# A new order for the first iterations, the routed rows in four parts, and a new order of iterations 13 and 14 in a gated-delta and expert layer

## The reference

```
mixed = silu(causal_conv(xn @ w_qkv))           # q, k: 16 heads; v: 32 heads, of 128
q, k = l2norm(q), l2norm(k); beta = sigmoid(xn @ w_b); g = -exp(A_log)*softplus(xn @ w_a + dt_bias)
step: St = St*exp(g); delta = (v - k.St)*beta; St = St + k delta; o = (q/sqrt(128)).St
attn = (rmsnorm(o)*norm_weight*silu(xn @ w_z)) @ w_out
ffn  = sum of 2 of 8 experts, weighted, + (silu(xn @ w_gate)*(xn @ w_up)) @ w_down   # shared, 1024 wide
out  = x + attn + ffn
```

## Time and profile before

| | us |
|---|---|
| three runs | 1098.22, 1091.68, 1098.17 (median 1098.17) |
| profiled execution, its own time | 1106.24 |
| its span, first to last instruction | 1104.3 |
| busy: TensorE / VectorE / ScalarE / GpSimd | 1030.0 / 800.5 / 633.9 / 519.3 |
| mean granted TensorE clock | 0.98 |

### The profile page before, as it was taken

The page is one execution under the profiler, slowest core; times in us unless marked ns, Lnnn a source line. Parts: engine busy times, 40 slices in busy tenths (PEclk is TensorE's granted clock), DMA queues, the critical chain, the costliest instruction groups (busy, mean ns, idle before and its releaser), DMA issues.

```text
span 1104.3 us, 22254 instructions
## 1 busy us (share of the span) xinstructions
PE 1030.0 (93%) x8190; PEld 789.7 (72%) x8190; DVE 800.5 (72%) x1469; ACT 633.9 (57%) x1176; POOL 519.3 (47%) x1140
## 2 busy tenths in 40 slices
PE   4889999999789999999999999999999999996897
PEld 4665666578476877777777778777777778783776
DVE  4552332275769898989889898989888988897444
ACT  4341222234557777666767576777767676774453
POOL 4500000266455557383847465564738374735610
PEclk9989999999879999999999999999999999998999
DMA  9933111151132333415152334233241514332121
GB/s 325 398 114 111 48 34 59 54 160 26 44 120 37 125 50 113 97 65 123 46 116 68 96 74 125 44 119 67 96 104 58 123 57 105 75 97 42 24 47 48
DMA packets 183513, 103.16 MB, mean 93 GB/s; under 512 B 155632, under 2 KB 169584, under 8 KB 180080
## 3 DMA queue, kind: packets, MB, share of 16 engines
q1 hardware_dynamic: 181872, 97.55, 32.1%
q0 software_dynamic: 1536, 4.20, 1.1%
HBM read 79.77 MB, written 21.95 MB: 92 GB/s over the span
## 4 chain that ended last, share of the span: by engine, by line
PE 57%; DVE 8%; ACT 7%; issue 4%; POOL 3%; DMA 1%; SPq 0%; ACTq 0%; DVEq 0%
PE rg L1585 9%; PE pj L1416 6%; PE pj L1418 5%; PE pj L1417 5%; PE rg L1568 5%; PE rg L1552 5%; PE rg L1486 4%; DVE nm L1294 3%; PE rg L1560 3%; PE rg L1569 2%; DVE shared_down_or_conv L1257 2%; ACT vn L1229 2%; ACT sqk L1183 2%; PE rg L1488 2%; PE rg L1531 2%
## 5 line engine op out<-in xcount | busy, mean ns | idle before, releaser
L1085 POOL TENSOR_TENSOR rows<-rows,shared_down_or_conv 128x126 f32<-128x126 f32 (+22 forms) x496 | 187.7, 378 | 239.1 <-DMA shared_down_or_conv<-n_scratch 201.5
L1257 DVE SCALAR_TENSOR_TENSOR shared_down_or_conv<-pj,taps,shared_down_or_conv 128x510 f32<-128x510 f32 x372 | 275.5, 744 | 27.5 <-ACT shared_down_or_conv L1135 18.8
L1088 POOL TENSOR_TENSOR rows<-rows 128x126 f32<-128x126 f32 (+22 forms) x496 | 194.8, 393 | 38.9
L1416 PE MATMUL pj<-xhi,whi 128*128 128x512 f32 x376 | 164.1, 437 | 2.4 <-POOL wlo L1065 1.4
L1294 DVE SCALAR_TENSOR_TENSOR nm<-rg,wneg,hidden_or_decays 128x512 f32<-128x512 f32 (+1 forms) x256 | 139.5, 609 | 15.9 <-PE rg L1488 14.1
L1418 PE MATMUL pj<-xhi,wlo 128*128 128x512 f32 x376 | 149.9, 399 | 0.0
L1417 PE MATMUL pj<-xlo,whi 128*128 128x512 f32 x376 | 149.8, 398 | 0.0
L1135 ACT ACTIVATE shared_down_or_conv<-pj,taps 128x512 f32<-128x512 f32 x124 | 85.0, 686 | 108.0 <-PE pj L1418 106.4
L1585 PE MATMUL rg<-wo,gated 128*128 128x256 f32 x512 | 130.6, 391 | 0.1
L1585 PEld LDWEIGHTS rg<-wo,gated 128*128 128x128 f32 x512 | 95.0, 192 | 15.1 <-issue 1.3
L1416 PEld LDWEIGHTS pj<-xhi,whi 128*128 128x128 f32 x376 | 71.5, 190 | 42.7 <-issue 24.4
(11 more groups left out here) (238 smaller groups left out, 1991.3 us busy)
## 6 DMA issues: line engine op xcount, KB each, us to landing
hidden_or_decays<-eg_scratch SPq DMA_DIRECT2D x16, 1536.0 KB, 8.0
wraw<-w_heads SPq DMA_DIRECT2D x16, 776.0 KB, 4.5
w1a<-w_up SPq DMA_DIRECT2D x9, 1024.0 KB, 7.7
shared_down_or_conv<-n_scratch SPq DMA_DIRECT2D x32, 256.0 KB, 4.0
w2a<-w_down SPq DMA_DIRECT2D x8, 512.0 KB
wo<-w_out SPq DMA_DIRECT2D x16, 256.0 KB
n_scratch<-nm SPq DMA_DIRECT2D x64, 64.0 KB
rt_scratch<-shared_down_or_conv SPq DMA_DIRECT2D x32, 128.0 KB, 2.3
```

The source lines that it names most:

```text
L1085: gp.tensor_tensor(tmp, rb[:, 0:r, t:t + 1].to_broadcast([P, r, w]), nb[:, t:t + 1, t + 1:].to_broadcast([P, r, w]), ALU.mult).then_inc(el ...
L1088: gp.tensor_tensor(rb[:, 0:r, t + 1:], rb[:, 0:r, t + 1:], tmp, ALU.add).then_inc(elim, 1)
L1257: v.scalar_tensor_tensor(out=y, in0=it.pbank[item][:, :, 0:S - s], scalar=taps[par][:, piece(j)[0], KS - 1 - s:KS - s], in1=y, op0=ALU.mul ...
L1416: te.matmul(bank, whi[par][w], xhi[:, k, cols], start=(k == 0), stop=False)
```

## The change

- Iteration -1: on TensorE, K3 moves ahead of H1 and VT0 to VT3 behind P3. D0 to D3 and E0 to E3 of group 1 are done here and not in iteration 0.
- The 16 row adds become MIX0 to MIX3 of four rows. The first three wait for 12 rows and stand in iteration -1, the last stands behind P4 of iteration 0. GpSimd fetches rows 5 to 11 in iteration -1 and rows 12 to 15 at the start of iteration 0, ahead of the weight split.
- Iteration 0 begins with SQ and K0 to K3, so K3 comes before P4; LA1 to LB2 stand between the first pieces.
- Iteration 13: K2 and K3 move ahead of LA1, and VectorE does D3 ahead of K1.
- Iteration 14: P5 to P7 stand between LA1, LA2, LB1 and LB2, and Z3 behind OUT5. P4's convolution moves behind K3 on VectorE.
- `blocks_out` of group 15 moves behind all of `blocks_back` of group 14, as in all other iterations.

```
+            FIRST_ROWS = 12
                 -1: (
-                    ("K0 G0 K1 H0 G1 K2 H1 K3 P4 G2 H2 P5 G3 H3 P6 DN0 P7 DN1 G4 H4 P0 VT0 VT1 G5 H5 P1 VT2 VT3 G6 H6 P2 "
-                     "G7 H7 P3 DN2 DN3").split(),
-                    ("G0 W G1 P4 G2 P5 S4 G3 P6 S5 SK P7 S6 G4 S7 P0 VT0 VT1 G5 P1 S0 VT2 VT3 G6 P2 S1 G7 P3 S2 S3").split(),
-                    ("K0 K1 H0 K2 H1 K3 P4 H2 P5 H3 P6 DN0 P7 DN1 H4 P0 H5 P1 H6 P2 H7 P3 DN2 DN3").split(),
+                    ("K0 K1 G0 K2 H0 K3 G1 H1 P4 G2 H2 P5 G3 H3 P6 DN0 P7 DN1 G4 H4 P0 G5 H5 P1 G6 H6 G7 H7 P2 P3 "
+                     "VT0 VT1 VT2 VT3 DN2 DN3").split(),
+                    ("G0 W G1 P4 G2 P5 S4 G3 P6 S5 SK P7 S6 G4 S7 P0 E0 G5 P1 S0 G6 S1 G7 P2 P3 E1 S2 VT0 VT1 VT2 VT3 "
+                     "S3 E2 E3").split(),
+                    ("K0 K1 K2 H0 K3 H1 P4 H2 P5 H3 P6 DN0 P7 DN1 H4 D0 P0 H5 MIX0 P1 H6 MIX1 H7 D1 P2 P3 D2 DN2 D3 MIX2 "
+                     "DN3").split(),
                 0: (
-                    ("Z0 Z1 P4 P5 SQ Z2 K0 P6 Z3 K1 K2 P7 P0 LA1 K3 LA2 LB1 P1 LB2 U1_0 U1_1 N21_0 N21_1 P2 U2_0 U2_1 "
-                     "VT0 P3 O0 VT1 O1 VT2 O2 O3 VT3").split(),
+                    ("SQ K0 Z0 K1 Z1 LA1 K2 Z2 LA2 K3 Z3 LB1 P4 LB2 P5 U1_0 U1_1 P6 N21_0 N21_1 P7 U2_0 U2_1 P0 O0 P1 O1 "
+                     "VT0 P2 VT1 P3 O2 O3 VT2 VT3").split(),
...
-                    ("D0 P4 D1 D2 P5 SQ D3 K0 P6 K1 K2 P7 K3 MIX N21_0 N21_1 P0 P1 P2 O0 P3 O1 O2 O3").split(),
+                    ("SQ K0 K1 K2 K3 P4 MIX3 P5 N21_0 N21_1 P6 P7 P0 O0 P1 O1 P2 P3 O2 O3").split(),
                 NG - 3: (
-                    ("SO Z0 P4 Z1 SQ Z2 K0 OUT0 K1 OUT1 Z3 OUT2 P5 P6 P7 LA1 K2 OUT3 LA2 K3 LB1 OUT4 OUT5 LB2 P0 OUT6 "
+                    ("SO Z0 P4 Z1 SQ Z2 K0 OUT0 K1 OUT1 Z3 K2 P5 K3 P6 OUT2 P7 LA1 OUT3 LA2 OUT4 LB1 OUT5 LB2 P0 OUT6 "
...
-                    ("D0 SO D1 SQ P4 K0 OUT0 OUT1 D2 K1 D3 OUT2 P5 K2 OUT3 K3 P6 OUT4 OUT5 P7 OUT6 N21_0 P0 N21_1 P1 P2 "
+                    ("D0 SO D1 SQ P4 K0 OUT0 OUT1 D2 D3 K1 K2 K3 OUT2 P5 OUT3 P6 OUT4 OUT5 P7 OUT6 N21_0 P0 N21_1 P1 P2 "
                      "OUT7 P3 O0 O1 O2 O3").split(),
                 NG - 2: (
-                    ("P4 Z0 SO SQ Z1 P5 K0 K1 K2 K3 LA1 Z2 OUT0 P6 OUT1 OUT2 Z3 OUT3 OUT4 LA2 P7 LB1 OUT5 OUT6 LB2 U1_0 "
-                     "U1_1 N21_0 N21_1 OUT7 U2_0 U2_1 VT0 VT1 O0 O1 O2 VT2 VT3 O3").split(),
+                    ("P4 Z0 SO SQ Z1 K0 K1 K2 K3 LA1 Z2 OUT0 LA2 P5 OUT1 LB1 P6 OUT2 LB2 P7 OUT3 U1_0 U1_1 N21_0 OUT4 "
+                     "N21_1 OUT5 Z3 U2_0 U2_1 OUT6 VT0 VT1 OUT7 O0 O1 O2 VT2 VT3 O3").split(),
...
-                    ("D0 D1 SO P4 SQ D2 D3 K0 K1 K2 K3 P5 OUT0 P6 OUT1 OUT2 OUT3 OUT4 OUT5 OUT6 N21_0 N21_1 P7 OUT7 O0 "
+                    ("D0 D1 SO D2 SQ D3 K0 K1 K2 K3 P4 OUT0 P5 OUT1 P6 OUT2 P7 OUT3 N21_0 OUT4 N21_1 OUT5 OUT6 OUT7 O0 "
                      "O1 O2 O3").split(),
@@ SyncE
                     turned_back(2, tc2, turned_in)
-                    if n == NG - 2:
-                        blocks_out(n + 1, 1 - it.odd)
                     sp.wait_ge(r_out, 32 * n + 32)
...
-                        if b != NG - 2:
-                            blocks_out(b + 1, 1 - it.odd)
+                        blocks_out(b + 1, 1 - it.odd)
@@ GpSimd
                     if it.b == -1:
                         gather(range(0, 5))
+                    elif it.b == 0:
+                        gp.wait_ge(gathered, FIRST_ROWS * 16)
+                        gather(range(FIRST_ROWS, 2 * NT))
+                        gp.wait_ge(gathered, 2 * NT * 16)
                     if "W" in it.items_a:
                         split_lo(it.b + 2, it.odd, it)
                     if it.b == -1:
-                        gather(range(5, 8))
-                    elif it.b == 0:
-                        gather(range(8, 2 * NT))
-                        gp.wait_ge(gathered, 2 * NT * 16)
+                        gather(range(5, FIRST_ROWS))
@@ VectorE
-                def combine():
+                def combine(some, added):
 
-                    v.wait_ge(gathered, 2 * NT * 16)
-                    v.wait_ge(v_free, WHERE["DN3"].v("DN3"))
-                    for i in range(2 * NT):
+                    v.wait_ge(gathered, (FIRST_ROWS if some.stop <= FIRST_ROWS else 2 * NT) * 16)
+                    v.wait_ge(v_free, WHERE[added].v(added))
+                    for i in some:
```

More of the change, by code:

```diff
@@ L840, in kind @@
             def kind(item):
-                return item.split("_")[0] if "_" in item else (item if item in ("LA1", "LA2", "LB1", "LB2", "SQ", "SK", "SO", "W", "MIX") else
+                return item.split("_")[0] if "_" in item else (item if item in ("LA1", "LA2", "LB1", "LB2", "SQ", "SK", "SO", "W") else
                                                                item.rstrip("0123456789"))
@@ L845, in build @@
             EARLY = {"W", "P0", "P1", "P2", "P3", "S0", "S1", "S2", "S3"}
[L846 removed]
+            FRONT = {"P", "S", "SQ", "SK", "K", "D", "E", "VT"}
             TAIL = {"SO", "OUT"}
[L848 removed]
+            LATER = {"G", "H", "DN", "MIX"}
             OWN = {
                 -1: (
[L851 to L861 removed]
@@ new lines, in build @@
+                0: (
+                    ("SQ K0 Z0 K1 Z1 LA1 K2 Z2 LA2 K3 Z3 LB1 P4 LB2 P5 U1_0 U1_1 P6 N21_0 N21_1 P7 U2_0 U2_1 P0 O0 P1 O1 "
+                     "VT0 P2 VT1 P3 O2 O3 VT2 VT3").split(),
+                    ("SQ Z0 Z1 LA1 Z2 LA2 Z3 LB1 W P4 LB2 P5 S4 U1_0 U1_1 SK P6 S5 U2_0 U2_1 P7 S6 P0 S7 O0 P1 S0 O1 VT0 "
+                     "P2 S1 VT1 P3 S2 O2 O3 VT2 S3 VT3").split(),
+                    ("SQ K0 K1 K2 K3 P4 MIX3 P5 N21_0 N21_1 P6 P7 P0 O0 P1 O1 P2 P3 O2 O3").split(),
@@ L871, in build @@
                 NG - 2: (
-                    ("P4 Z0 SO SQ Z1 P5 K0 K1 K2 K3 LA1 Z2 OUT0 P6 OUT1 OUT2 Z3 OUT3 OUT4 LA2 P7 LB1 OUT5 OUT6 LB2 U1_0 "
-                     "U1_1 N21_0 N21_1 OUT7 U2_0 U2_1 VT0 VT1 O0 O1 O2 VT2 VT3 O3").split(),
-                    ("P4 SQ SO E0 Z0 E1 S4 Z1 P5 E2 E3 LA1 S5 P6 Z2 Z3 LA2 SK LB1 LB2 U1_0 U1_1 U2_0 P7 S6 U2_1 S7 VT0 "
-                     "O0 O1 VT1 O2 VT2 VT3 O3").split(),
-                    ("D0 D1 SO P4 SQ D2 D3 K0 K1 K2 K3 P5 OUT0 P6 OUT1 OUT2 OUT3 OUT4 OUT5 OUT6 N21_0 N21_1 P7 OUT7 O0 "
+                    ("P4 Z0 SO SQ Z1 K0 K1 K2 K3 LA1 Z2 OUT0 LA2 P5 OUT1 LB1 P6 OUT2 LB2 P7 OUT3 U1_0 U1_1 N21_0 OUT4 "
+                     "N21_1 OUT5 Z3 U2_0 U2_1 OUT6 VT0 VT1 OUT7 O0 O1 O2 VT2 VT3 O3").split(),
+                    ("SQ P4 SO E0 Z0 E1 Z1 E2 E3 LA1 S4 Z2 LA2 P5 LB1 P6 S5 LB2 P7 S6 U1_0 U1_1 SK S7 Z3 U2_0 U2_1 VT0 "
+                     "VT1 O0 O1 O2 VT2 VT3 O3").split(),
+                    ("D0 D1 SO D2 SQ D3 K0 K1 K2 K3 P4 OUT0 P5 OUT1 P6 OUT2 P7 OUT3 N21_0 OUT4 N21_1 OUT5 OUT6 OUT7 O0 "
                      "O1 O2 O3").split(),
@@ L896, in present @@
                     def present(order):
-                        return [i for i in order if kind(i) in LATER or not (b == -2 or b == -1 and (kind(i) in ("D", "E") or i == "SQ")) and (b <= NG - 3 and (b > -2 or i != "W") if i in EARLY else
+                        return [i for i in order if kind(i) in LATER or not (b == -2 or b == -1 and i == "SQ") and (b <= NG - 3 and (b > -2 or i != "W") if i in EARLY else
                                                      -1 <= b <= NG - 2 if kind(i) in FRONT else
@@ L1331, in run @@
                         k = kind(item)
-                        if item == "MIX":
-                            combine()
+                        if k == "MIX":
+                            i = number(item)
+                            combine(range(4 * i, 4 * i + 4), "DN1" if 4 * i + 4 <= FIRST_ROWS else "DN3")
                         elif k == "H":
@@ L1342, in run @@
                         elif k == "D":
-                            decays(n, number(item))
+                            decays(max(n, 1), number(item))
                         elif k == "K":
```

10 lines of the change are left out of this document (3 added, 7 removed).

## The result

The changed kernel takes 1077.42 us (median of 4 runs, 1074.4 to 1083.04); the kernel before took 1096.38 beside it (4 runs, 1091.68 to 1098.22). The ratio is 0.984, with a 95% interval of 0.981 to 0.987. The forecast was 1078, a ratio of 0.982. The profiled execution of after took 1083.04 with a span of 1081.1, against 1106.24 and 1104.3 before.

What follows compares the result with a forecast made beforehand. TensorE's own work was taken to bound the middle, with slow stretches around iteration 0 and behind LA1 of iteration 14. Front 13.6 plus tail 6.0 made 19.6 off the 1098.17 median: 1078 us, range 1067 to 1091.

Steps and rivals of the forecast that it cites:

- The front: Iterations -1 and 0: work moved, none removed; SQ of iteration 1 comes 13.6 us earlier, bounds 4 and 16.
- the slow stretch: DN3 to SQ of iteration 1, 63.67 us: eight GpSimd gathers delay VectorE and ScalarE; clock at 1.2 GHz around LA1.
- the slow stretch is LA1's and returns: Rival, iteration 0: the gathers aren't the cause, so the slow stretch comes back; gain 9.7, 1088 us, chance 0.17.
- MIX beside the elimination: Iteration -1: row adds and GpSimd's elimination exclude each other; group 0's rows 2 us later, still before LA1 needs them.
- Iteration 13: K3's product ends 5.1 us earlier; LB2 and all behind it come about 2 us later on TensorE.
- Behind LA1 of 14: TensorE's part behind LA1 of iteration 14 takes 32.8 us against 40.7, which is 7.9 less.
- the step: Tail: LA1 of iteration 15 waits for group 15's blocks and elimination, so 8.5 us earlier, not 13; TensorE stands 4.5.
- The clock behind LA1 of 15: TensorE comes back at 1.2 GHz after its wait before LA1 of iteration 15; priced at 2.5 us.
- The tail: Iterations 13 to 15: 8.5 less 2.5 for the clock, a gain of 6.0 us, bounds 2 and 10.
- VectorE didn't become the bound in the front: Rival, iterations -1 and 0: VectorE becomes the bound through MIX and decays; 5 us lost, 1083, chance 0.10.
- the orders act: Rival, iteration 13: the orders don't act, K3 is held by its bank, nothing of 5.1 left; 1084, chance 0.02.
- the slower case: Rival, iteration -1: MIX0 waits for twelve rows; each us past 257 costs one; 1109 us, chance 0.03.

Runs made afterwards that it cites:

- gathers_early: Kernel before with one edit: in iteration 0 GpSimd fetches the eight rows and waits for them before it splits the weights. Ratio 0.997.
- again: The changed kernel unaltered, timed a second time beside the kernel before: 1088.27 us, ratio 0.9822.
- tail alone: Kernel before with only the lists of iterations 13 and 14 and the place of the last blocks_out changed. Ratio 0.9936.
- eight_late: Changed kernel with gathers divided as in the kernel before, eight in one run at the start of iteration 0, MIX2 moved there too: 1087.04 us.

## Why the prediction was right

- **The front** was given 13.6 and measured 14.5 (14.9 when alone). Its terms: DN3 ends 1.1 us later against the first key product, for 0.8; the idle time before SQ was 1.43, for 1.6; and iteration 0 from SQ to SQ took 46.48 (266.83 to 313.31), for 46.2 + 1.4. The reason stated for the slow stretch holds by half. The gathers do hold up LA1's chain (four of them beside LA1: 3.8 us), but in the old order the clock falls without them too. And that the remaining gathers are harmless beside large matmuls was too simple: in gathers_early eight of them, beside DN products and pieces, cost 3.1 us ahead of SQ. The four of the new order cost nothing that shows. The rival "the slow stretch is LA1's and returns" is refuted for the new order, where nothing is below full clock near it, and is half right for the old one.
- **MIX beside the elimination.** The row adds take 2.44 and 2.27 per four beside it, 1.65 free of it, and the elimination of group 0 takes 30.26 for 28.33. That is the rule of the Trainium skill, SBUF — State Buffer, section "SBUF: two separate sides", which the prediction weighed (VectorE with two SBUF inputs and GpSimd reading SBUF exclude each other); the trace agrees in sign and in the 2 us, and as forecast LA1 of iteration 0 doesn't feel it: the rows land 3.5 us before it.
- **Iteration 13.** K3's product ends at 947.43; that is 5.25 us earlier against SO of iteration 13 than before, for 5.1 forecast. K3's second bank waits for K1, as written: TensorE's 1.37 idle at 942.59. LA1 of iteration 14 is 5.05 earlier (5.1), the stall 4.30 (about 3): TensorE is there 1.0 us earlier than before with P5 moved behind, so the lateness that I put at 2 was 0.5. This is the firm part of the tail: from SO of iteration 13 to LA1 of iteration 14 it takes 74.2 to 74.9 in the three traces with the old order and 68.8 to 69.5 in six with the new.
- **Behind LA1 of 14** TensorE's work takes 43.07 us to where it stands again (993.80 to 1036.87), forecast 41.4; the idle of 3.19 is that much less than the 4.5. LA1 to LA1 is 46.26, forecast 45.9. What holds LA1 of 15 is the serial chain over the elimination, as the step said; that elimination took 28.47, below the 29.2 taken, but from the issue of the blocks to its start it is 10.4 for 9.2, and two wrong sizes nearly cancel. The gain behind LA1 of 14 is less sure than it looks: the 49.33 that the forecast started from is 46.8 and 46.6 in the other two traces with the old tail, which have 10.2 us at 0.50 around LA1 of 14 for 13.7, and none at VT, though TensorE is idle 3.38 there as well.
- **The clock behind LA1 of 15** was priced at 2.5. It cost 3.8, 2.3 and 0 in three executions (after, again, tail alone) against the 37.23 before. Over the six traces with this tail and no useless work the mean is 1.8, so the term is near the mean but has no fixed size. Nor does it follow the idle time alone: 2.13 (eight_late) cost 2.3 and 2.16 (tail alone) nothing.
- **The tail** was given 6.0: 4.3, 6.0, and 8.7 when alone, all against the one trace of before, whose 161.0 is the longest of the three old tails.
- **What the sum left out** is the middle. "There TensorE's own work is the bound and nothing on the other engines is worth removing" was half right: in before TensorE idles only 0.3 us an iteration at LA1, but LA1 already starts at the landing in most iterations. With the new front the transfers of the loop take 0.5 us longer in sum and the elimination 0.15, of which the 0.3 us between landing and LA1 take up a part, and the middle grew by 3.2 and 5.5 us where I counted none. So the traces show 13.4 and 17.6 us of the 19.6, while the medians show 19. Over the traces with the new front and the old middle orders, from LA1 of iteration 1 to that of 12, an iteration takes 50.9 to 51.5 us; with the old front, 50.9 to 51.0. So the effect isn't there in every execution. Why the transfers are slower stays open; no run isolates it.
- **The number.** The median came out 0.6 us from the 1078. That closeness is luck: a term of 3 to 5 us was put at nothing, the tail's terms vary by several us between executions, and the interval of the ratio alone is about 3.6 us to each side. Carrying over the 8.1 us by which the profiled execution was slower than the median was sound in kind: most of it fits the part ahead of the first key product, which the change leaves alone and which is 9.8 us shorter in after. What the runs bear out is the mechanism: the front's terms, the 5 us of iteration 13, and the elimination of group 15 as the next thing that is late.
- **The other rivals.** VectorE didn't become the bound in the front (14.9 gained), the orders act (K3's 5.25), and the slower case needed rows past 257: the seventh gather was issued by 229.5 and MIX0 began at 246.02 (239.3 and 255.8 by the times of before, whose first part is 9.8 longer).
